# A graph layer with aggregation on one core: one loop for all rounds, two 128-column groups per step, x loaded into the output's place

## The reference

```python
agg = jax.ops.segment_sum(edge_attr, dst, num_segments=6250)
h = jnp.concatenate([x, agg, u[batch]], axis=1)      # batch is 0 for every node
h = jax.nn.relu(h @ W1 + b1)
y = h @ W2 + b2
out = layernorm(x + y)                               # over the 128 features, eps 1e-5
```

## Time and profile before

| | us |
|---|---|
| median of 3 runs | 280.54 |
| lowest and highest | 279.39 and 281.53 |
| the profiled execution | 281.41 |
| its span, first to last instruction | 279.6 |
| PE busy (share of span) | 214.6 (77%) |
| VectorE busy | 167.3 (60%) |
| ScalarE busy | 51.3 (18%) |
| GpSimd busy | 40.8 (15%) |
| moved by DMA | 110.06 MB, mean 394 GB/s |

### The profile page before, as it was taken

How to read it: one execution, slowest core, us unless ns; L and a number is a source line. 1 busy time by engine, 2 the same in 40 slices (tenths; PEclk the granted TensorE clock), 3 DMA queues, 4 the chain that set the end, 5 groups by cost and what they waited for, 6 DMA issues and landing times.

```text
span 279.6 us, 15292 instructions
## 1 busy us (share of the span) xinstructions
PE 214.6 (77%) x6763; PEld 168.8 (60%) x6763; DVE 167.3 (60%) x425; ACT 51.3 (18%) x99; POOL 40.8 (15%) x49
## 2 busy tenths in 40 slices
PE   0978699687786786696877799898876867767992
PEld 0866577556655665575555677677655655655761
DVE  7952565783774665655773426959565464687352
ACT  0511022211211220220210211322221121110210
POOL 6400020120210300400401100303020030011020
PEclk9987999999999999999995679999999999997998
DMA  7999999999999999999999999999999999999992
GB/s 254 345 359 398 401 399 401 401 400 401 402 399 402 401 401 401 402 399 414 416 412 411 415 416 417 414 416 418 414 419 413 420 416 415 409 419 413 414 390 83
DMA packets 30843, 110.06 MB, mean 394 GB/s; under 512 B 2197, under 2 KB 3370, under 8 KB 30826
## 3 DMA queue, kind: packets, MB, share of 16 engines
q1 hardware_dynamic: 27508, 105.83, 95.3%
q10 hardware_dynamic: 3318, 4.00, 4.2%
HBM read 106.63 MB, written 3.20 MB: 393 GB/s over the span
## 4 chain that ended last, share of the span: by engine, by line
PE 55%; DMA 21%; issue 16%; DVE 2%; ACTq 2%; POOL 1%; ACT 1%; DVEq 0%; POOLq 0%
PE rows_ps L803 30%; DMA slots<-in_edge_attr 18%; PE cols_ps L815 14%; DMA rest_slot<-in_edge_attr 4%; PE hid_ps L847 3%; PE hid_ps L829 3%; PE hid_ps L838 2%; PE hid_ps L823 1%; ACT rows L411 1%; POOL rstd L375 1%; DVE stats L622 1%; DVE z L637 0%; PE hid_ps L929 0%; PE rows_ps L896 0%; POOL z L366 0%
## 5 line engine op out<-in xcount | busy, mean ns | idle before, releaser
L803 PE MATMUL rows_ps<-slots,hot 64*32 64x128 f32 x6240 | 113.7, 286 | 40.4 <-issue 38.0
L803 PEld LDWEIGHTS rows_ps<-slots,hot 64*32 64x32 f32 x6240 | 93.9, 110 | 59.4 <-issue 57.7
L600 DVE TENSOR_TENSOR agg_t<-agg_t,cols_ps 128x128 f32 (+1 forms) x65 | 21.6, 332 | 89.4 <-PE cols_ps L815 89.3
L574 DVE TENSOR_TENSOR hot<-edge_node,iota 128x768 f32<-128x768 f32 x65 | 62.0, 953 | 12.6 <-issue 9.8
L815 PE MATMUL cols_ps<-row_hot,rows 128*128 128x128 f32 (+1 forms) x260 | 55.8, 339 | 10.6 <-ACT rows L411 5.7
L411 ACT ACTIVATE rows<-rows_ps 128x256 f32<-128x256 f32 x65 | 24.9, 383 | 182.7 <-PE rows_ps L803 178.7
L815 PEld LDWEIGHTS cols_ps<-row_hot,rows 128*128 128x128 f32 x260 | 40.5, 197 | 24.3 <-issue 12.3
L375 POOL TENSOR_TENSOR rstd<-var_eps,minus_half 128x4 f32<-128x4 f32 (+1 forms) x13 | 16.6, 1275 | 205.3 <-DVE var_eps L631 205.3
L590 DVE TENSOR_TENSOR row_hot<-row_node,iota 128x256 f32<-128x256 f32 (+1 forms) x65 | 37.4, 576 | 0.0
L366 POOL TENSOR_TENSOR z<-x_rows,b_all 128x512 f32<-128x512 f32 (+1 forms) x13 | 16.5, 1268 | 27.8 <-PE hid_ps L823 27.8
L637 DVE TENSOR_SCALAR z<-z,moments,rstd (+1 forms) x49 | 16.9, 403 | 0.9 <-POOL rstd L375 0.9
(11 more groups left out here) (106 smaller groups left out, 63.2 us busy)
## 6 DMA issues: line engine op xcount, KB each, us to landing
slots<-in_edge_attr SPq DMA_DIRECT2D x65, 1536.0 KB, 17.8
x_rows<-in_x ACTq DMA_DIRECT2D x11, 256.0 KB
out<-z SPq DMA_DIRECT2D x11, 256.0 KB
dst_int<-in_dst SPq DMA_DIRECT2D x1, 384.0 KB, 3.9
dst_int<-in_dst ACTq DMA_DIRECT2D x1, 384.0 KB, 4.5
x_rows<-in_x ACTq DMA_DIRECT2D x1, 192.0 KB
out<-z SPq DMA_DIRECT2D x1, 192.0 KB
rest_slot<-in_edge_attr ACTq DMA_DIRECT2D x1, 160.0 KB, 10.0
```

The costliest lines, as they stand in the source:

```text
L574: V.tensor_tensor(hot[i][:, :, :], edge_node[:, bass.ds(t, 1), :, :].rearrange("p o c r -> p (o c r)").unsqueeze(2).broadcast_to([P, RUNS, ...
L600: V.tensor_tensor(cols, cols, cols_ps[:, 0:n], ALU.add).then_inc(added, 1)
L803: done = T.matmul(rows_ps[i][c * SPAN:(c + 1) * SPAN, h, 0:feats], hot[j][part, c * RUN + r, :], slots[part, j, c, r * feats:(r + 1) * fea ...
```

## The change

- **One loop.** `one_lap` takes the place of `sparse_lap` and `dense_lap` on TensorE and VectorE. Every step is level 1, then (in some steps) one product of the node block, then level 2 of the same step. There is one pair of banks `rows_ps` and one `rows`.
- **Two groups of 128 columns.** Level 2 is done for two halves of the partitions with tiles of 64 rows, each half into a bank of its own and with a base of its own. `row_hot` is 128 wide in every step. VectorE makes two additions of 128 columns per step, the second waits for the first.
- **Order on VectorE.** In a step the addition comes first, then the part of the node block, then the one-hots of step t+3. They are made without a condition in lap 12 too (steps 65, 66 and 67, from zeroed entries of the tables).
- **x into the output's place.** ScalarE's queue loads x into `z`; ScalarE copies it to `x_rows` (`stage_x`), from where TensorE turns it. GpSimd's addition is gone. b2 comes in as a product of one row of ones with four copies of b2 (`bias2`, 512 columns), into a bank of its own that the products with W2 then add to. Turned x, hidden layer and y have a bank each. The product of x with W1 is done one lap earlier, in step 3 of its own lap.
- **Blocks** begin at node 128, so that one block at the top is short (490 nodes) and the last is nodes 0 to 127, as before.
- **u and b1 as rows.** They are loaded in one piece each; u is turned by a product, b1 is added by a product.
- **Rest of the edges.** The 320 first edges are handled in lap 11 (one-hots, before `judge`) and lap 12 (products in step 60, addition in step 62). The three filling products are gone.

```diff
@@ VectorE
-            def add(t, at, dense_step):
+            def add(t, at):
                 dve.wait_ge(level2_done, t + 1)
-
-                dve.wait_ge(added, t + 1)
-                n = DENSE_COLS if dense_step else COLS
-                cols = agg_t[:, bass.ds(at, n)]
-                V.tensor_tensor(cols, cols, cols_ps[:, 0:n], ALU.add).then_inc(added, 1)
+                for g in range(GROUPS):
+
+                    dve.wait_ge(added, t * GROUPS + (g + 1))
+                    cols = agg_t[:, bass.ds(at[g], COLS)]
+                    V.tensor_tensor(cols, cols, cols_ps[:, g, 0:COLS], ALU.add).then_inc(added, 1)
...
+            def one_lap(lap):
                 at = counts(lap)
                 for j in range(LAP):
                     t = lap * LAP + j
...
+                    add(t, at[j * GROUPS:(j + 1) * GROUPS])
+                    if not isinstance(lap, int):
+                        if j == 1:
+                            residual(lap - 1, lap - 1)
+                            with dve.If(lap == laps - 2):
+                                make_rest_hot()
+                                judge()
+                        elif j == 2:
+                            variance(lap - 1, lap - 1)
+                            with dve.If(lap > laps - 2):
+                                make_plan()
+                                add_rest(t)
+                        elif j == 3:
+                            normalise(lap - 1, lap - 1)
+                    make_hot(t + AHEAD, j + AHEAD)
```

```diff
@@ TensorE
-            def level2(t, j, dense_step):
-                i, n = SETS[j], DENSE_COLS if dense_step else COLS
-                pe.wait_ge(rows_copied, t + 3)
+            def level2(t, j):
+
+                pe.wait_ge(added, t * GROUPS + 1)
                 pe.wait_ge(row_hot_made, t + 1)
-
-                pe.wait_ge(added, t + 1)
+                pe.wait_ge(rows_copied, t + 1)
                 for h in range(HALVES):
-                    done = T.matmul(cols_ps[:, 0:n], rows[i][:, h, :], row_hot[j][:, h, 0:n], start=(h == 0), stop=(h == HALVES - 1))
+                    for g in range(GROUPS):
+                        part = slice(g * HALF, (g + 1) * HALF)
+                        done = T.matmul(cols_ps[:, g, 0:COLS], rows[part, h, :], row_hot[j][part, h, :], start=(h == 0), stop=(h == HALVES - 1),
+                                        tile_position=(g * HALF, 0))
                 done.then_inc(level2_done, 1)
...
+            def one_lap(lap):
                 counts(lap)
                 for j in range(LAP):
                     t = lap * LAP + j
                     level1(t, lap, j)
 
-                    if j:
...
+                    if j == 0:
                         with pe.If(lap > 0):
...
+                            pe.wait_ge(added, t * GROUPS + 1)
                             product1_agg(lap - 1, start_of(lap - 1))
+                            bias2(lap - 1, lap - 1)
+                        with pe.If(lap > final - 1):
+                            rest_and_bounds()
+                    elif j == 1:
                         with pe.If(lap > 0):
                             product2(lap - 1, lap - 1)
+                    elif j == 2:
+                        turn_x(lap)
                     elif j == 3:
...
+                        product1_x(lap, BLOCK)
+                    level2(t, j)
```

```diff
@@ ScalarE, start
             act.dma_start(dst_int[:, HALVES:2 * HALVES, :], dst_pairs[1]).then_inc(dst_in, 16)
-
-            act.sem_inc(rows_copied, 2)
+            act.dma_start(u_row[:, :], u[0:1, :]).then_inc(u_in, 16)
+            act.dma_start(w1u[:, :], w1[2 * feats:2 * feats + ufeats, :]).then_inc(u_in, 16)
+            act.dma_start(b1_row[:, :], b1.rearrange("(a c) -> a c", a=1)).then_inc(u_in, 16)
+            act.dma_start(b2_row[:, :], b2.rearrange("(a c) -> a c", a=1)).then_inc(u_in, 16)
+            act.wait_ge(z_zero, 1)
+            load_x(0)
             act.dma_start(w1x[:, :], w1[0:feats, :]).then_inc(w_in, 16)
             act.dma_start(w1a[:, :], w1[feats:2 * feats, :]).then_inc(w_in, 16)
-            act.dma_start(w1u[:, :], w1[2 * feats:2 * feats + ufeats, :]).then_inc(w_in, 16)
             act.dma_start(w2_sb[:, :], w2).then_inc(w_in, 16)
-            act.dma_start(u_col[:, :], u[0:1, :].rearrange("a c -> c a")).then_inc(w_in, 16)
-            act.dma_start(b1_col[:, :], b1.rearrange("(c a) -> c a", a=1)).then_inc(w_in, 16)
```

More of the change, by code:

```diff
@@ L154, in residual_gnn_layer @@
         row_hot = [sb(f"row_hot{i}", [P, HALVES, COLS]) for i in range(HOTS)]
-        rows = [sb(f"rows{i}", [P, HALVES, feats]) for i in range(3)]
+        rows = sb("rows", [P, HALVES, feats])
         agg_t = sb("agg_t", [P, width])
@@ L284, in general_if, with x_landed @@
             return eng.value_load(plan[0:1, 0:1], min_val=0, max_val=1)
-        weights = 7
+        weights = 3
         pieces = places + 2
-        def x_landed(seq):
-            turns, i = seq // places, seq % places
-            return 16 * (turns * pieces + i + 1 + (2 if i >= short else 0))
+        def x_landed(turns, i):
+            return i * 16 + 16 * (turns * pieces + 3)
         @block.sync
@@ L678, in sparse_lap @@
                     t = lap * LAP + j
-                    mixed = not isinstance(lap, int) and j + AHEAD >= LAP
-                    make_hot(t + AHEAD, j + AHEAD, None if mixed else False)
-                    add(t, at[j], False)
-                    if isinstance(lap, int):
-                        continue
-                    if j == 2:
-                        residual(lap - 1, lap - 1)
-                    elif j == 3:
-                        variance(lap - 1, lap - 1)
-                    elif j == 4:
-                        normalise(lap - 1, lap - 1)
@@ L692, in dense_lap @@
-            def dense_lap(lap):
-                at = counts(lap)
-                for j in range(LAP):
-                    t = lap * LAP + j
-                    if j + AHEAD < LAP:
-                        make_hot(t + AHEAD, j + AHEAD, True)
-                    else:
-                        with dve.If(lap < laps - 1):
-                            make_hot(t + AHEAD, j + AHEAD, True)
-                    add(t, at[j], True)
-                    if j == 1:
-                        residual(lap - 1, lap - 1)
-                        with dve.If(lap == laps - 2):
-                            judge()
-                    elif j == 2:
-                        variance(lap - 1, lap - 1)
-                        with dve.If(lap > laps - 2):
-                            make_plan()
-                    elif j == 3:
-                        normalise(lap - 1, lap - 1)
+                    add(t, at[j * GROUPS:(j + 1) * GROUPS])
@@ L839, in product1_agg, with bias2 @@
-                done.then_inc(hid_done, 1)
-            def start_of(i):
-                return 0 if isinstance(i, int) and i == final else (blocks - 1) * BLOCK - i * BLOCK
+                n = rows_of(i) * P
+                T.matmul(hid_ps[:, 0:n], w1a[:, :], agg_t[:, bass.ds(at, n)], start=False, stop=True).then_inc(hid_done, 1)
+            def bias2(seq, i):
+                pe.wait_ge(row_node_made, GROUPS)
+                pe.wait_ge(b2_made, 1)
+                pe.wait_ge(z_made, seq + 1)
+                n = rows_of(i) * feats
+                T.matmul(y_bank[:, 0:n], ones[0:1, :], b2_rows[:, :, :].rearrange("a r f -> a (r f)")[:, 0:n], start=True, stop=False)
@@ L846, in product2 @@
                 for r in range(rows_of(i)):
-                    done = T.matmul(y_ps[:, r, :], hid[:, r * P:(r + 1) * P], w2_sb[:, :], start=True, stop=True)
+                    done = T.matmul(y_ps[:, r, :], hid[:, r * P:(r + 1) * P], w2_sb[:, :], start=False, stop=(r == rows_of(i) - 1))
                 done.then_inc(y_done, 1)
@@ L957, in _ @@
                 done.then_inc(ids_turned, 1)
-            with pe.Fori(0, DENSE_LAP) as lap:
-                sparse_lap(lap)
-            level2(DENSE - 1, LAP - 1, False)
-            with pe.Fori(DENSE_LAP, laps) as lap:
-                dense_lap(lap)
-            pe.wait_ge(added, steps + 1)
+            pe.wait_ge(u_made, 1)
+            T.matmul(bias_ps, w1u[:, :], u_col[:, :], start=True, stop=False)
+            T.matmul(bias_ps, b1_row[:, :], ones[0:1, 0:1], start=False, stop=True).then_inc(bias_done, 1)
+            with pe.Fori(0, laps) as lap:
+                one_lap(lap)
+            bias2(final, final)
+            pe.wait_ge(added, steps * GROUPS + 1)
             product1_agg(final, start_of(final))
```

405 lines of the change are left out of this document (164 added, 241 removed).

## The result

The change makes the kernel slower: 289.67 us (median of 6, from 288.67) against 281.03 us for the kernel before beside it, a ratio of 1.0311 [1.0277, 1.0345]. The profiled execution took 288.67 us with a span of 286.9; the profiled one of before 281.41 and 279.6. So 7.3 us of span have to be found.

A forecast was written before the change was run, and what follows sets the result against it. The prediction took the DMA loads as the bound, hiding the steady laps. Tail 0.7 plus clock 0.5 less head 0.15 gave about +1.0 us: profiled 282.4, median 281.5, range 278.5 to 285.

The forecast's parts named there:

- clock term: Tail: TensorE's clock falls behind the pause at 247.9, some 4 us earlier than before; 0.5 us lost, bounds 0 to 1.5.
- head term: Head: u and b1 as rows spare 192 small packets, 0.3 us of transfer; half of it, 0.15 us, counted as gain.
- Level 1 of step 60 at 254.0: Tail: after level 2 of step 59, level 1 of step 60 begins at 254.0, much as before.
- From 274.03 on the same short chain follows in both kernels: End: behind the last block's product the same chain runs in both kernels, 5.6 us to the end of the span.
- The cover of 12 us: Laps 1 to 10: over four queued loads hide TensorE's delays until it falls some 12 us behind.
- the 380 foreseen: Head, window 10 to 11 us: the profile after would show over 380 GB/s.
- I take 0.7: Every step: level 2 with eight instructions costs 0.7 us, between 0.45 side by side and 0.9 in turn.
- that rival: Level 2's halves run one after the other, 0.9 us instead of 0.7 in seven steps, +1.4 us; 283 to 285, chance 0.13.
- Step 60's load of extra products: Lap 12, step 60: W1, b2, ten rest products and three of the bounds, with level 2 done at 260.3.
- Level 1 of step 64 to the last product: End: level 1 of step 64 at 269.4, last product at 274.75, additions held up by one-hots nobody reads, 2.6 us.
- about 2: Lap 11: TensorE waits about 2 us, 247.9 to 249.9, for the additions of step 57 behind `judge`.
- the clock makes TensorE the bound: Rival, laps 1 to 10: half clock at stops pushes TensorE's lap past the loads' 20.2 us; over 286, chance 0.09.

The follow-up runs named there:

- a_checks_early: Changed kernel with `judge` and the one-hots of the rest done in lap 3 instead of lap 11: 283.87 us, 1.0132.
- a_b2_all_rows: Changed kernel with the b2 product done with all 128 rows, 127 of them zeros, instead of one: 284.48 us, 1.0178.
- a_no_spare: Changed kernel without the one-hots of steps 65 to 67 in lap 12: 287.01 us, 1.0213.
- a_hots_first: Changed kernel with the one-hots of step t+3 made ahead of the additions of step t, as before the change: 289.64 us, 1.0323.
- a_rest_only: Changed kernel with the rest's one-hots in lap 3 and their ten products in lap 4, checks and bounds unmoved: 285.17 us, 1.018.
- a_no_b2: Changed kernel with b2 left out of the sum, W2's products starting y themselves: 283.45 us, 1.0112.
- a_again: The changed kernel run once more, unedited: 288.18 us, 1.0236.
- a_best: Changed kernel with checks, rest and bounds early, no one-hots of steps 65 to 67, last product with x 128 columns wide: 280.86 us, 1.0007.
- a_best_hots_first: `a_best` with the one-hots of step t+3 made ahead of the additions of step t: 279.58 us, 0.9955.
- b_checks_early: Kernel before with `judge` in lap 7 instead of lap 11: 279.42 us, 0.9953; run again, 278.43 us, 0.9967.
- b_checks_rows: Kernel before with `judge` in lap 7 and u and b1 loaded as rows: 279.0 us, 0.994; run again, 278.3 us, 0.9953.

## Why the prediction was wrong

The forecast's span was 280.6 us; it became 286.9. Of the 6.3 us, 2.8 are a second fall of the clock, 2.3 the late start of step 60 (the forecast's clock term, less its head term, had 0.35 of them), and 1.6 the exit.

**The step that failed most is the clock term**: "I take 0.5, bounds 0 to 1.5." It counted one fall, behind the pause, and took over the size of before's. For that fall it holds: about 0.5, 0.9 at most. What it left out is a second fall in step 60, worth about 2.8 us (2.9 and 3.1 against `a_checks_early` and `a_b2_all_rows`). The prediction had all its ingredients in the same sentence ("b2, the ten products of the rest ..., the three of the bounds") and priced them by their time alone. Profiles with the pause in lap 11, the rest's products and the one-row product of b2 (the changed kernel twice, `a_no_spare`, `a_hots_first`) have the fall, four of four, 4.6 to 5.0 us after step 60 begins. Where one of them is changed it is absent: the checks moved (`a_checks_early`), the rest's products moved (`a_rest_only`), the b2 product left out (`a_no_b2`) or given 128 rows (`a_b2_all_rows`). The times side with the traces: with all three, 14 of the 15 executions in the ratios took over 286 us; of `a_rest_only` and `a_b2_all_rows`, two of eight did.

So it is firm that the fall sits in this stretch and costs its 2.8 us. That each of the three is needed is not shown. Each of the four variants was traced once, and each edit also shifts the step in time. A rival stands untested: whether the clock falls may hang on the moment at which the same work is done, which differs from one execution to the next, as `a_again` shows for the first fall and for those of the covered laps. (The second doesn't hang on the first: `a_again` and `a_hots_first` lack the first and have the second.) Several traces of each variant would decide. Why products such as these bring it no run here shows.

**Level 1 of step 60 at 254.0, "much as before"**, was 2.3 us too early. Step 55 lets the lateness in. In it stand both extra products, W1's and the new one of b2, and the chain of waits of after goes from its level 1 over W1 to level 1 of step 56, 4.4 us for one load's 3.8:

```profile
234.23 1.58 PE rows_ps L769 x95
235.85 1.12 PE hid_ps L801 x2
238.67 1.52 PE rows_ps L769 x96
```

I had put step 56 where its load lands, at 237.8. So `judge` ended 0.8 us later (248.8 for 248.0), the first fall added 0.5 to level 2 of step 58 and 1.1 to level 1 of step 59, and 0.44 us of waiting stood at the head of the lap; of these 2.8 some 0.5 were absorbed, where TensorE would have waited for VectorE anyway. In `a_again`, without the first fall, it is 255.84 all the same, since there `judge` ended later still (249.3) and level 2 of step 59 waited 1.29 us for the additions of step 58. This is VectorE's queue, not the clock. (Two slips of the working change nothing: the product with x stands in step 58, at 247.07 and ahead of the pause, not in step 59; and the terms of TensorE's lap add up to 16.8 us, not 16.9.)

**"From 274.03 on the same short chain follows in both kernels"**: to the end of the last normalise it does (3.5 us in both). The exit doesn't, 3.65 us against 1.98, so 1.7 us that no term had. SyncE's waits in the last 5 us, of after and of before:

```profile
SPq L102 <- PEq L102: 1.2, 1, 1.2
```

```profile
SPq L96 <- PEq L96: 0.2, 1, 0.2
```

These 1.0 us go with the one-hots that nobody reads. In the three kernels without them (`a_no_spare`, `a_best`, `a_best_hots_first`) the wait is as short as before, in all others made from the changed one it is 0.5 to 1.2 us. The line of `a_no_spare`:

```profile
SPq L102 <- PEq L102: 0.2, 1, 0.2
```

The other 0.7 us are SyncE's wait for the last store of the output, of after and of before:

```profile
SPq L102 <- DMA out<-z: 1.8, 1, 1.8
```

```profile
SPq L96 <- DMA out<-z: 1.1, 1, 1.1
```

It is 1.8 to 2.1 us in all kernels made from the changed one and 1.1 to 1.7 in those from before. Altogether the exit is 2.6 to 3.7 us in the first and 2.0 to 2.5 in the second. By what way the one-hots lengthen TensorE's end, and why the store's wait is longer, no run here shows.

**The cover of 12 us** is not there in every lap (`b_checks_early` ran it low in lap 7). In laps 0 and 1 the queue of loads isn't full yet, and it ran nearly dry:

```profile
42.00:49.00 7.00, 4.89 (x118) 2.59 (x114) 1.87 (x5) 1.07 (x2) 0.00 (x0) 1.00 1.00 364
49.00:56.00 7.00, 7.00 (x290) 6.04 (x294) 4.76 (x12) 2.44 (x4) 0.00 (x0) 1.00 0.95 359
```

That is 364 and 359 GB/s where before had 401 over both windows: 0.55 MB less, or 1.4 us. It used up what the head had gained: the window 12 to 16 went from 290 to 336 GB/s. The window 10 to 11 went from 335 to 353 only, not to the 380 foreseen. `a_no_b2` has 388 and 407 in the two windows of the dip, but `a_b2_all_rows`, with a b2 product as long, has 386 and 392, and `a_again` has 381 and 359: the length of that product doesn't explain it, and the cause stays open. What the loads lose in the dip they don't make up by the tail. Level 1 of step 55 starts in all these kernels where its load lands (the row names the DMA), at 234.23 in the changed kernel and here in `a_no_b2`:

```profile
232.58 1.58 PE L769 MATMUL rows_ps<-slots,hot 64*32 64x128 f32 x96 [1.05 <-DMA slots<-in_edge_attr]
```

So these two executions differ by 1.6 us of loads. By my count from the last landing (268.3 less nine loads of 3.8) it would have been at 234.1: the loads of the changed kernel are on before's time, with head and dip cancelling. The other variants are at 233.42 (`a_b2_all_rows`), 233.83 (`a_checks_early`), 234.70 (`a_again`) and 235.82 (`a_rest_only`). When their last products are compared, this has to be taken off. `a_b2_all_rows` is 4.4 us ahead of the changed kernel at the last product, of which 0.8 are loads; `a_rest_only` is 3.5 ahead although its loads are 1.6 late.

**What held.** The rates of the middle are the same. Level 2 with eight instructions takes 0.71 us ("I take 0.7"), behind the copy or not; in the chain's measure it is 0.65 to 0.67 where other products cover the copy, for 0.45 before and 0.9 if the halves ran in turn. So that rival is out; the halves overlap, though not wholly. The Trainium skill's statement (TensorEngine Tiling, Key Properties) that tiles load and multiply in parallel agrees with the row that far. Step 60's load of extra products took 6.5 us for 6.3, which is partly luck: 0.5 of it are the second fall, and at full clock it is 5.9 (`a_checks_early`). Level 1 of step 64 to the last product is 5.34 us for 5.35, with the additions of step 64 directly behind one-hots 66, as foreseen. TensorE waited 2.5 us for the additions of step 57, for "about 2". The rival "the clock makes TensorE the bound" had the right resource in the wrong place: in laps 0 to 10 the clock did fall, for 3.4 us at a time in the changed kernel, and never made TensorE the bound of the middle; in lap 12 it did, with 3 us and not 10. "Over 286" was its time, and its chance of 0.09 was too small because the pause was looked at and what TensorE does between two pauses wasn't.

## What to carry to other kernels

In a kernel bound by its loads, price an edit where the cover ends, in the last lap and in the first two; in the middle it cost next to nothing here. Work that is done once (checks, remainders) belongs in a lap with cover: moving the checks was worth 5.4 us of span in the changed kernel (286.9 to 281.5) and 0.3 to 0.5% in the one before. Look at the loads' rate in the lap that takes it: lap 3 took it without a dip, lap 7 didn't. `b_checks_rows` has the lowest ratio of all versions, 0.994 and 0.995, but `b_checks_early` and `a_best_hots_first` can't be told from it. When summing TensorE's queue, look in the trace for half clock in stretches without a pause as well: in lap 12, where one-row products and products of few columns stand together, it cost 2.8 us more than their own time.

## What the runs showed of the hardware

- The granted clock fell to 0.51 at 261.0, behind 4.7 us in which TensorE was busy for 4.65. The Trainium skill (TensorE: Matmul & The Clock Gate, What's actually happening) says that the gate goes by how busy TensorE has been; busy time as the profile counts it doesn't show it here. With the same product of b2 made of 128 rows (596 ns) in place of one (640 ns) the one profile taken went without the fall.
- A pause brings the fall in some executions and not in others, whatever its length between 1.9 and 2.5 us. It did with 2.5 us (changed kernel), 2.4 (`a_b2_all_rows`), 2.1 (`a_no_spare`), 2.0 (before) and 1.95 (`a_no_b2`). It didn't with 2.5 (`a_hots_first`), 2.1 (`a_rest_only`) and 1.9 (`a_again`).
- While the clock was down the loads went on at 409 to 419 GB/s. The kernel before spent 13.6 us of its middle at half clock, at 410 and 413 GB/s, without losing time by it.
